# Scores of the second sequence and value products at other steps of TensorE's program

## Chip, cores and metric

The kernel runs on one core of one Trainium2 chip. The metric is the device time of one execution in microseconds (us), as the median of several runs. The profile is that of one further execution.

## The reference

A layer of a small transformer with 32 sequences of 256 tokens and width 128. A layer norm without scale feeds two branches whose results are added to `x`:

```
xn = layernorm(x)
h  = relu(xn @ nm_w1 + nm_b1);  m = h @ nm_w2 + nm_b2
q, k, v = m @ q_w + q_b, m @ k_w + k_b, m @ v_w + v_b
attention: softmax over the keys within 32 positions of the query, scale 1/sqrt(128)
scores = sigmoid(xn @ gate_w.T);  the 8 best of 16 experts by scores + expert_bias,
         their scores divided by their sum, times 2.826
y  = sum over experts of combine * (silu(xn @ w_gate.T) * (xn @ w_up.T)) @ w_down.T
y += the same for a shared expert, with weight 1
out = x + attention + y
```

All is float32. All 16 experts are computed for all tokens, and the combine weights of those not chosen are zero.

## The kernel before

**Tiles.** Tokens are worked in 16 groups of 512, two sequences each. Tensors lie transposed, 128 features on the partitions and 512 tokens along the row. To keep float32 precision each operand is split in two parts in TensorE's float32r type, `hi` (a copy that rounds) and `lo` (what is left), and each product is made of three, `PAIRS3`: hi by hi, hi by lo, lo by hi.

**Steps.** A group is 17 steps (`STEPS`), one for the shared expert and one for each of the 16. Each engine has its own program, written out by hand as `slot(g, par, s)`, and all five are tied by semaphores alone. The expert of step s goes through:
- PE (TensorE): gate product `ps_g` (L370, one step ahead), up product `ps_u` (L380), later the down product into `ps_y` (L390), `LAG` = 3 steps behind. Each is three products of 512 columns.
- ACT (ScalarE): `silu` of `ps_g` (L564), one step ahead; `h_hi` from `ps_u` (L572), one step behind.
- POOL (GpSimd): `silu_c`, the silu times the combine weight (L969).
- DVE (VectorE): `ps_u` times `silu_c` in place (L889) and `h_lo` (L895), one step behind.

There are two buffers each for `ps_g` and `ps_u`. So the gate product of step s waits for the silu of step s-2 (L368), and the up product of step s, called up(s) in the prediction, waits for `h_lo` of step s-2 (L378).

**The attention of the group** and the router and hidden layer of the next one are laid between these steps. On PE `att_early` stands between the gate product and the down product, `att_late` between the down product and the up product, and step 7 has something behind the up product. For this case they matter in this order:
- step 1: transposes of the next group's `xn` into `bank[1]`
- step 3: `scores(0)`, six products of 160 columns into `score_bank[0]` = `bank[2]`, with ahead of it the wait for `q_lo` (L459)
- step 4: `gate(1 - par)`, the router products of the next group, eight of 32 columns into `bank[0]` (L318), with ahead of it the waits for `xn_lo`, `hn_lo` and `key_term`
- step 5: `scores(1)`, the same into `score_bank[1]` = `bank[1]` (L329)
- step 7: four transposes of the probabilities of sequence 0 (L338), then the hidden projection of the next group (L306); step 9: the transposes of sequence 1
- step 13: `attend(0)`, step 14: `attend(1)`, the value products of the two sequences, six products of 160 or 256 columns each, into two halves of `bank[2]` (L348); the second raises `pv`

The other engines: DVE takes the row maximum of sequence 0 in step 4 and that of sequence 1 at the very start of step 6 (`row_max`, L810). ACT has in step 5 the exponential of the router and of sequence 0, in step 6, between `h_hi` of step 5 and the silu of step 7, the exponentials of sequence 1 (L553). Exponential and silu need a table load between them. DVE normalises the probabilities in steps 6 and 8 (L818, L822), ahead of that step's `h_lo`. ACT waits for `pv` in step 15 (`z_hi`, L547).

Of the kernel before, what the change touches and what calls it, by code (L numbers as in the profile page):

```python
# [64 lines left out]
def layer(nc, x, x_t, watt, watt_t, expert_bias, wexp, out_t, c_dram):  # L65
    ctx = ExitStack()
    with ctx:
# [6 lines left out]
        def sem(name):  # L74
            return ctx.enter_context(nc.semaphore(name))
# [120 lines left out]
        S = {n: sem(n) for n in names}  # L196
# [13 lines left out]
        def first(g):  # L210
            return g == 0

        def last(g, ahead=0):
            return g >= GROUPS - 1 - ahead
# [9 lines left out]
        def flat(t):  # L224
            return t[:].rearrange("p a d -> p (a d)")
# [75 lines left out]
        def _(pe):  # L301
# [7 lines left out]
            def turn(dst, src):  # L309
                for a in range(TILES):  # L310
                    done = nc.tensor.transpose(dst[:, a * P:(a + 1) * P], src[:, a * P:(a + 1) * P], ident[:])  # L311
                return done

            def gate(par):

                for a in range(TILES):
                    for n in range(2):
                        done = mm(bank[0][:, a * 2 * E:(a + 1) * 2 * E], xn_t[par][n][:, a * P:(a + 1) * P],  # L318
                                  gate_w[:], start=n == 0, stop=n == 1)
                done.then_inc(S["gate_mm"], 1)  # L320

            def scores(seq):

                dst = score_bank[seq]
                for t in range(2):
                    q0 = seq * SEQ + t * P
                    k0 = seq * SEQ + t * (P - HALF)
                    for n, (a, b) in enumerate(PAIRS3):
                        done = mm(dst[:, t * SEQ:t * SEQ + WIN], q_t[a][:, q0:q0 + P], hid_t[b][:, k0:k0 + WIN],  # L329
                                  start=n == 0, stop=n == 2)  # L330
                done.then_inc(S[f"sc{seq}"], 1)

            def turn_probs(seq):
                dst = score_bank[seq]
                for kb in range(2):
                    for t in range(2):
                        c = kb * (SEQ - (P - HALF)) + t * P
                        done = nc.tensor.transpose(dst[:, c:c + P],  # L338
                                                   prob_n[:, 2 * seq + t, kb * P:(kb + 1) * P], ident[:])
                done.then_inc(S[f"pt{seq}"], 1)  # L340

            def attend(seq):

                for kb in range(2):
                    col = seq * SEQ + kb * (P - HALF)
                    for n, (a, b) in enumerate(PAIRS3):
                        wide = SEQ if kb == 0 and n == 0 else WIN
                        done = mm(bank[2][:, col:col + wide], hid_n[a][:, seq * 2 + kb, :],  # L348
                                  p_t[b][:, seq, kb, 0:wide], start=kb == 0 and n == 0, stop=kb == 1 and n == 2,
                                  skip_group_check=True)  # L350
                return done

            def value_proj(g):

                pe.wait_ge(S["z_lo"], g + 1)
                for a, b in PAIRS3:
                    mm(ps_y[:], att_w[a][:, 2, :], z_t[b][:], start=False, stop=False, skip_group_check=True)  # L357
# [42 lines left out]
            def q_proj(g):  # L400
                pe.wait_ge(S["hid_lo"], g + 1)
                project(bank[1], 1, hid_t).then_inc(S["q_mm"], 1)

            def hid_turn(g):

                pe.wait_ge(S["hid_lo"], g + 1)
                turn(bank[0], hid).then_inc(S["hid_tp"], 1)
# [40 lines left out]
            def att_early(g, par, s):  # L448

                more = not last(g)  # L450
                if s == 1 and more:
                    pe.wait_ge(S["xn"], g + 2)

                    pe.wait_ge(S["q_lo"], g + 1)
                    turn(bank[1], flat(xn)).then_inc(S["xn_tp"], 1)
                if s == 3:
                    if not first(g):
                        pe.wait_ge(S["z_lo"], g)
                    pe.wait_ge(S["q_lo"], g + 1)  # L459
                    scores(0)  # L460
                if s == 4 and more:
                    pe.wait_ge(S["xn_lo"], g + 2)

                    pe.wait_ge(S["hn_lo"], g + 1)
                    pe.wait_ge(S["key_term"], 2 * g + 2)
                    gate(1 - par)
                if s == 5:
                    scores(1)
                if s == 15 and more:
                    q_proj(g + 1)  # L470
                if s == 16 and more:
                    hid_turn(g + 1)

            def att_late(g, par, s):

                if s == 0 and not first(g):
                    value_proj(g - 1)
                if s == 9:
                    pe.wait_ge(S["pn1"], g + 1)
                    turn_probs(1)  # L480
                if s == 13:
                    pe.wait_ge(S["hn_lo"], g + 1)
                    pe.wait_ge(S["p0_lo"], g + 1)
                    attend(0)
                if s == 14:
                    pe.wait_ge(S["p1_lo"], g + 1)
                    attend(1).then_inc(S["pv"], 1)

            def slot(g, par, s):
                if first(g) and s == 0:  # L490
                    gate_proj(g, par, s)
                if not (last(g) and s == STEPS - 1):
                    gate_proj(*after(g, par, s))
                att_early(g, par, s)
                if not first(g) or s >= LAG:
                    down(*before(g, par, s, LAG))
                att_late(g, par, s)
                up_proj(g, par, s)
                if s == 7:
                    pe.wait_ge(S["pn0"], g + 1)  # L500
                    turn_probs(0)
                    if not last(g):
                        hid_proj(g + 1, 1 - par)
# [510 lines left out]
```

## Time and profile before

| | us |
|---|---|
| median of 3 runs | 722.94 (722.91 to 723.25) |
| profiled execution | 722.1 |
| its span | 720.2 |
| PE busy | 701.5 (97% of the span) |
| DVE busy | 574.2 (80%) |
| ACT busy | 438.9 (61%) |
| POOL busy | 399.7 (55%) |

Busy time is the union of an engine's instructions. Products on PE are pipelined: one is shown with about 0.4 us, but the next begins 0.23 us after it. So the distance between starts tells what a product costs, and not its duration. Instructions of DVE and ACT overlap by about 0.1 us in the same way. In brackets behind an instruction stands how long its engine idled before it and which instruction ended that.

### The profile page before, as it was taken

What the parts mean: (1) busy time and instruction counts of PE and PEld (TensorE: products, weight loads), DVE (VectorE), ACT (ScalarE), POOL (GpSimd) and SP (SyncE); (2) the same over time, 40 slices, a digit from 0 to 9 for tenths busy, and PEclk for the clock granted to TensorE, in tenths of its full rate; (3) what the DMA queues carried; (4) which work ended last, traced back from release to release, by engine and by line L of the source; (5) the groups of instructions that cost most, each with busy time, mean ns of one, the idle gap of its engine ahead of it and who ended that gap; (6) DMA issues with size and microseconds to landing.
All of it is one profiled execution on the core that took longest, in us unless ns stands there. A gap on an engine that the chain in (4) does not pass through costs nothing.

```text
span 720.2 us, 10617 instructions
## 1 busy us (share of the span) xinstructions
PE 701.5 (97%) x3384; PEld 577.2 (80%) x3384; DVE 574.2 (80%) x1605; ACT 438.9 (61%) x874; POOL 399.7 (55%) x356
## 2 busy tenths in 40 slices
PE   5889999999999999999999999999999999999997
PEld 4667888888888888888888888888888888888886
DVE  4788788787888878788887888878787887878775
ACT  3575665666656575665766656566655766656573
POOL 3745555546565555565556655555565555655463
PEclk9999999999999999999999999999999999999999
DMA  7704316061250615216061340615215061430600
GB/s 256 256 10 152 130 26 226 29 235 45 90 191 2 234 45 177 103 47 218 16 235 45 109 172 4 236 42 204 76 51 227 4 236 45 130 135 7 244 1 15
DMA packets 36647, 84.72 MB, mean 118 GB/s; under 512 B 7152, under 2 KB 15472, under 8 KB 36592
## 3 DMA queue, kind: packets, MB, share of 16 engines
q1 hardware_dynamic: 36592, 84.05, 33.2%
q8 instruction: 27, 0.44, 0.3%
q14 instruction: 28, 0.23, 0.1%
HBM read 79.32 MB, written 4.72 MB: 117 GB/s over the span
## 4 chain that ended last, share of the span: by engine, by line
PE 93%; DVE 3%; DMA 2%; ACT 1%; issue 0%; POOL 0%; SPq 0%; DVEq 0%
PE ps_y L390 26%; PE ps_u L380 26%; PE ps_g L370 26%; PE bank L348 3%; PE bank L306 3%; PE bank L329 3%; PE bank L318 2%; PE bank L311 2%; PE bank L338 2%; PE ps_y L357 1%; DMA comb_b<-c_dram 1%; DVE ps_u L889 0%; DVE h_lo L895 0%; DVE exp_w_lo L644 0%; DMA xin<-x 0%
## 5 line engine op out<-in xcount | busy, mean ns | idle before, releaser
L969 POOL TENSOR_TENSOR silu_c<-silu,comb_b 128x512 f32<-128x512 f32 x256 | 330.5, 1294 | 300.7 <-ACT silu L564 297.1
L572 ACT ACTIVATE h_hi<-ps_u 128x512 fp32r<-128x512 f32 x272 | 162.5, 598 | 261.7 <-DVE ps_u L889 259.8
L895 DVE TENSOR_TENSOR h_lo<-ps_u,h_hi 128x512 fp32r<-128x512 f32 x272 | 185.7, 683 | 59.9 <-ACT h_hi L572 59.7
L889 DVE TENSOR_TENSOR ps_u<-silu_c,ps_u 128x512 f32<-128x512 f32 x256 | 176.6, 690 | 44.5 <-PE ps_u L380 38.2
L564 ACT ACTIVATE silu<-ps_g 128x512 f32<-128x512 f32 x272 | 161.4, 594 | 0.2
L380 PE MATMUL ps_u<-xn_hi,exp_w_hi 128*128 128x512 f32 x272 | 110.7, 407 | 5.1 <-DVE h_lo L895 5.1
L390 PE MATMUL ps_y<-h_hi,exp_w_hi 128*128 128x512 f32 x272 | 112.7, 414 | 0.4 <-DVE h_lo L895 0.4
L370 PE MATMUL ps_g<-xn_hi,exp_w_hi 128*128 128x512 f32 x272 | 108.3, 398 | 0.0
L370 PE MATMUL ps_g<-xn_lo,exp_w_hi 128*128 128x512 f32 x272 | 108.0, 397 | 0.0
L370 PE MATMUL ps_g<-xn_hi,exp_w_lo 128*128 128x512 f32 x272 | 107.6, 395 | 0.0
L380 PE MATMUL ps_u<-xn_lo,exp_w_hi 128*128 128x512 f32 x272 | 107.5, 395 | 0.0
L390 PE MATMUL ps_y<-h_hi,exp_w_lo 128*128 128x512 f32 x272 | 107.5, 395 | 0.0
L390 PE MATMUL ps_y<-h_lo,exp_w_hi 128*128 128x512 f32 x272 | 107.2, 394 | 0.0
L380 PE MATMUL ps_u<-xn_hi,exp_w_lo 128*128 128x512 f32 x272 | 107.2, 394 | 0.0
L380 PEld LDWEIGHTS ps_u<-xn_hi,exp_w_hi 128*128 128x128 f32 x272 | 51.3, 189 | 17.3 <-DVE h_lo L895 7.3
L370 PEld LDWEIGHTS ps_g<-xn_hi,exp_w_hi 128*128 128x128 f32 x272 | 51.4, 189 | 12.5 <-issue 0.3
L370 PEld LDWEIGHTS ps_g<-xn_hi,exp_w_lo 128*128 128x128 f32 x272 | 51.4, 189 | 12.4
L390 PEld LDWEIGHTS ps_y<-h_hi,exp_w_lo 128*128 128x128 f32 x272 | 51.0, 188 | 12.5
L380 PEld LDWEIGHTS ps_u<-xn_hi,exp_w_lo 128*128 128x128 f32 x272 | 51.1, 188 | 12.2
L370 PEld LDWEIGHTS ps_g<-xn_lo,exp_w_hi 128*128 128x128 f32 x272 | 51.3, 189 | 11.9
L380 PEld LDWEIGHTS ps_u<-xn_lo,exp_w_hi 128*128 128x128 f32 x272 | 51.4, 189 | 10.0
L390 PEld LDWEIGHTS ps_y<-h_hi,exp_w_hi 128*128 128x128 f32 x272 | 51.3, 189 | 9.5 <-DVE h_lo L895 0.8
(139 smaller groups left out, 982.0 us busy)
## 6 DMA issues: line engine op xcount, KB each, us to landing
comb_b<-c_dram SPq DMA_DIRECT2D x64, 1024.0 KB, 8.7
xin<-x SPq DMA_DIRECT2D x16, 256.0 KB, 3.1
xres<-x_t SPq DMA_DIRECT2D x16, 256.0 KB, 2.7
out_t<-xres SPq DMA_DIRECT2D x16, 256.0 KB, 2.0
exp_raw<-wexp SPq DMA_DIRECT2D x3, 960.0 KB, 9.3
c_dram<-comb_t SPq DMA_DIRECT2D x64, 8.0 KB, 1.8
exp_raw<-wexp SPq DMA_DIRECT2D x1, 384.0 KB, 5.4
att_raw<-watt SPq DMA_DIRECT2D x1, 330.5 KB, 3.4
```

The costliest lines, as they stand in the source:

```text
L306: done = mm(dst[:], att_w[a][:, w, :], parts[b][:], start=n == 0, stop=n == 2)
L311: done = nc.tensor.transpose(dst[:, a * P:(a + 1) * P], src[:, a * P:(a + 1) * P], ident[:])
L329: done = mm(dst[:, t * SEQ:t * SEQ + WIN], q_t[a][:, q0:q0 + P], hid_t[b][:, k0:k0 + WIN], start=n == 0, stop=n == 2)
L348: done = mm(bank[2][:, col:col + wide], hid_n[a][:, seq * 2 + kb, :], p_t[b][:, seq, kb, 0:wide], start=kb == 0 and n == 0, stop=kb == 1 a ...
L370: done = mm(ps_g[i][:], exp_w[a][:, s, 0:P], xn_t[par][b][:], start=n == 0, stop=n == 2)
L380: done = mm(ps_u[i][:], exp_w[a][:, s, P:2 * P], xn_t[par][b][:], start=n == 0, stop=n == 2)
L390: done = mm(ps_y[:], exp_w[a][:, s, 2 * P:3 * P], h_t[i][b][:], start=s == 0 and n == 0, stop=s == STEPS - 1 and n == 2, skip_group_check= ...
L564: A(silu[i][:], ps_g[i][:], ACT.Silu).then_inc(s_silu, 1)
L572: A(h_t[hbuf(par, s)][0][:], ps_u[(par + s) % 2][:], ACT.Copy).then_inc(s_h_hi, 1)
L889: V.tensor_tensor(ps_u[i][:], src[:], ps_u[i][:], ALU.mult).then_inc(s_h, 1)
L895: V.tensor_tensor(t[1][:], ps_u[(par + s) % 2][:], t[0][:].bitcast(F32), ALU.subtract)\
L969: G.tensor_tensor(silu_c[i][:].rearrange("p (l x) -> p l x", l=2), silu[i][:].rearrange("p (l x) -> p l x", l=2), comb_b[:, :, s1 - 1, :], ...
```

## The change

In PE's program `scores(1)` moves from step 5 to step 4, where it stands directly behind the router products of the next group. `attend(0)` moves from step 13 to step 14, with its two waits, and now stands directly ahead of `attend(1)`; the wait for `p1_lo` is made ahead of both. The other engines' programs are the same as before.

```
@@ att_early
                     pe.wait_ge(S["hn_lo"], g + 1)
                     pe.wait_ge(S["key_term"], 2 * g + 2)
                     gate(1 - par)
-                if s == 5:
+                if s == 4:
                     scores(1)
@@ att_late
-                if s == 13:
+                if s == 14:
                     pe.wait_ge(S["hn_lo"], g + 1)
                     pe.wait_ge(S["p0_lo"], g + 1)
+                    pe.wait_ge(S["p1_lo"], g + 1)
                     attend(0)
-                if s == 14:
-                    pe.wait_ge(S["p1_lo"], g + 1)
                     attend(1).then_inc(S["pv"], 1)
```

## Rows read from the trace of the kernel before

**Rows 1.** The page: busy us of an engine, and TensorE's granted clock in 40 slices

```profile
PE 701.5 (97%) x3384; PEld 577.2 (80%) x3384; DVE 574.2 (80%) x1605; ACT 438.9 (61%) x874; POOL 399.7 (55%) x356
PEclk9999999999999999999999999999999999999999
```

**Rows 2.** Who waited for whom: us in total, times, longest us

```profile
PE ps_u L380 <- DVE h_lo L895: 5.1, 5, 2.7
```

**Rows 3.** Timeline (start us, us, engine line, operation), PE, group 2, steps 4 and 5

```profile
124.89 0.39 PE L370 MATMUL ps_g<-xn_hi,exp_w_lo 128*128 128x512 f32 x1
...
126.24 0.40 PE L390 MATMUL ps_y<-h_lo,exp_w_hi 128*128 128x512 f32 x1
...
127.17 0.39 PE L380 MATMUL ps_u<-xn_hi,exp_w_lo 128*128 128x512 f32 x1
...
127.87 0.40 PE L370 MATMUL ps_g<-xn_hi,exp_w_lo 128*128 128x512 f32 x1
...
129.00 0.40 PE L390 MATMUL ps_y<-h_lo,exp_w_hi 128*128 128x512 f32 x1
```

**Rows 4.** Timeline, PE, around `attend(0)` in step 13 of group 2

```profile
147.59 0.40 PE L390 MATMUL ps_y<-h_hi,exp_w_lo 128*128 128x512 f32 x1
...
148.73 0.39 PE L380 MATMUL ps_u<-xn_lo,exp_w_hi 128*128 128x512 f32 x1
```

**Rows 5.** Timeline, DVE, group 2: product of step 4 to `h_lo` of step 8

```profile
127.60 0.69 DVE L889 TENSOR_TENSOR ps_u<-silu_c,ps_u 128x512 f32<-128x512 f32 x1 [0.83 <-PE ps_u L380]
...
129.57 0.32 DVE L810 CUSTOM_DVE_ANT_0 prob<-bank,mask_k 128x160 f32<-128x160 f32 x1
...
131.84 0.17 DVE L818 RECIPROCAL row_inv<-row_sum 128x2 f32<-128x2 f32 x1 [0.78 <-ACT prob L553]
...
132.48 0.68 DVE L895 TENSOR_TENSOR h_lo<-ps_u,h_hi 128x512 fp32r<-128x512 f32 x1
...
140.36 0.68 DVE L895 TENSOR_TENSOR h_lo<-ps_u,h_hi 128x512 fp32r<-128x512 f32 x1
```

**Rows 6.** Timeline, ACT, group 2: `h_hi` of step 4 to the silu of step 7

```profile
128.33 0.60 ACT L572 ACTIVATE h_hi<-ps_u 128x512 fp32r<-128x512 f32 x1 [1.79 <-DVE ps_u L889]
...
129.44 1.28 ACT L528 ACT_TABLE_LOAD   x1
130.73 0.26 ACT L528 ACTIVATE gate_e<-gate_s 128x64 f32<-128x64 f32 x1
...
134.43 0.60 ACT L564 ACTIVATE silu<-ps_g 128x512 f32<-128x512 f32 x1
```

**Rows 7.** Timeline, group 0: `h_lo` of step 8 ends and up(10) begins

```profile
54.65 0.68 DVE L895 TENSOR_TENSOR h_lo<-ps_u,h_hi 128x512 fp32r<-128x512 f32 x1
...
55.38 0.19 PEld L380 LDWEIGHTS ps_u<-xn_hi,exp_w_hi 128*128 128x128 f32 x1 [0.72 <-DVE h_lo L895]
...
55.72 0.39 PE L380 MATMUL ps_u<-xn_lo,exp_w_hi 128*128 128x512 f32 x1
```

**Rows 8.** Timeline, PE, group 2: up(7), gate product of step 9, up(10); up(7) of group 3

```profile
133.67 0.39 PE L380 MATMUL ps_u<-xn_hi,exp_w_hi 128*128 128x512 f32 x1
...
135.51 0.40 PE L370 MATMUL ps_g<-xn_hi,exp_w_hi 128*128 128x512 f32 x1
...
141.53 0.39 PE L380 MATMUL ps_u<-xn_hi,exp_w_hi 128*128 128x512 f32 x1
...
176.71 0.39 PE L380 MATMUL ps_u<-xn_hi,exp_w_hi 128*128 128x512 f32 x1
```

**Rows 9.** Timeline, group 0: end of up(4) and DVE's product of step 4

```profile
36.95 0.40 PE L380 MATMUL ps_u<-xn_hi,exp_w_lo 128*128 128x512 f32 x1
...
37.86 0.68 DVE L889 TENSOR_TENSOR ps_u<-silu_c,ps_u 128x512 f32<-128x512 f32 x1
```

**Rows 10.** Timeline, group 15: silu of step 7 and gate product of step 9

```profile
692.40 0.60 ACT L564 ACTIVATE silu<-ps_g 128x512 f32<-128x512 f32 x1
...
693.38 0.40 PE L370 MATMUL ps_g<-xn_lo,exp_w_hi 128*128 128x512 f32 x1
```

More of the change, by code:

```diff
@@ L466, in att_early @@
                     gate(1 - par)
-                if s == 5:
+                if s == 4:
                     scores(1)
@@ L480, in att_late @@
                     turn_probs(1)
-                if s == 13:
+                if s == 14:
                     pe.wait_ge(S["hn_lo"], g + 1)
                     pe.wait_ge(S["p0_lo"], g + 1)
+                    pe.wait_ge(S["p1_lo"], g + 1)
                     attend(0)
-                if s == 14:
-                    pe.wait_ge(S["p1_lo"], g + 1)
                     attend(1).then_inc(S["pv"], 1)
```

## The prediction

> **What bounds the kernel now.** I read the page first: PE is busy for 701.5 us of the 720.2 us span, at a granted clock of 9 tenths or more in every slice, that is at the higher of its two levels, 2.4 GHz [rows 1]. Then I read who waits for whom. PE's only repeated wait is for `h_lo` of L895, before an up product: 5 times, 5.1 us [rows 2], and the timeline puts all five of them in group 0. From group 1 to group 14 the products follow each other without a hole. So PE's program order sets the time, and an edit there can act in two ways: by making the sum of PE's work shorter, or by opening a hole where an operand comes too late. The third view is therefore the timeline of one middle group (group 2), PE beside DVE and ACT. Steps are called s as in the code. The start of a product in a stalled or narrow place is taken as the start of the next product less 0.233 us, the spacing of wide (512 column) products: from 127.17 to 127.87 there are three spacings, 0.70 us [rows 3].
>
> **Part 1, PE's own work.** Nothing is added or removed: six narrow products per sequence for scores and six for values, in another place. What could change is the edge between wide and narrow products, since two blocks of 8 and 6 become one of 14, and two of 6 become one of 12. The eight router products: from the last wide start before them (124.89) to the second wide start behind them (126.24) is 1.35 us, less two wide spacings (0.467) makes 0.883. The six of the scores: 127.87 to 129.00 is 1.13, less 0.467 makes 0.663 [rows 3]. The two extra products cost 0.220, or 0.110 each; six at 0.110 leave 0.003 for the edges. Value products: 147.59 to 148.73 is 1.14, less 0.467 makes 0.673 [rows 4], of which 6 x 0.110 leaves 0.013. An edge thus costs between nothing and about 0.015 us. Two edges less in 16 groups give 0 to 0.5 us; I take 0, as a difference of rows rounded to 0.01 can't carry more.
>
> Here a rule of the Trainium skill can be weighed. "TensorE: Matmul & The Clock Gate", section "Back-to-back issue gap", gives a sustained spacing of about 81 ns for products of 128 columns. By it six narrow products would take an estimated 0.49 us, and the sum below would come out at about 725.7 instead of 728.4 (rival C). The rows show 0.110 us each, whether the product has 32 or 160 columns, so the rule does not hold for these float32 operands.
>
> **Part 2, what the moved scores delay.** In step 4 the order becomes gate product of step 5, the eight router products, scores(1), down of step 1, up of step 4. So up(4) ends 0.66 us later. Step 5 gets the same 0.66 us shorter, so the gate product of step 6 starts 0.66 later, and up(5) and all of PE behind it start as now. scores(1) itself adds no wait in this place: the semaphores that it relies on have been waited for by scores(0) and by the router products. Its own reader, the row maximum of sequence 1, stands in DVE's step 6 and starts at 129.57 with no wait ahead of it, behind `h_lo` of step 4 [rows 5]; it comes by DVE's order and not by the scores' end, so nobody gains from having them early.
>
> Who waits for up(4) is what counts. DVE's product of step 4 starts at 127.60 after 0.83 us of idleness that up(4) ended [rows 5]; up(4) ends at 127.17 + 0.39 [rows 3]. So it moves by the whole 0.66, to 128.26. ACT's `h_hi` of step 4 starts at 128.33 after 1.79 us of waiting for that DVE product, and moves to 128.99. Behind it ACT has no hole up to silu(7): silu(6), a table load, the exponentials of both sequences with `h_hi` of step 5 between them, a second table load, silu(7) at 134.43 [rows 6]. ACT is in order, so silu(7) ends at 135.03 + 0.66 = 135.69. On DVE the probabilities of sequence 0 wait for the exponentials (131.84, 0.78 us idle), and `h_lo` of step 5 (132.48, ends 133.16) [rows 5] stands behind them: it ends at 133.82. From there DVE has at most short holes, each ended by ACT or by POOL, which itself waits for silu(7), up to `h_lo` of step 10. So `h_lo` of step 8 (ends 141.04) [rows 5] is 0.66 later too.
>
> Another rule of the Trainium skill speaks of the table loads. "ScalarE: Activation LUTs", section "What ACT_TABLE_LOAD costs", adds a drain of about 1380 ns to every load. By it ACT would have no slack to PE at all, and all 0.66 us would come through in each group (rival B). The row shows 1.28 us from 129.44 and the next instruction at 130.73 [rows 6], so no drain is seen.
>
> **Part 3, how much slack PE has.** Where PE really waited, in group 0, `h_lo` ended at 55.33, the weight load began at 55.38, and the second product at 55.72, so the first counts from 55.49: an operand must be there 0.16 us before the product's start [rows 7]. With that, from group 2:
> - up(7) starts at 133.67 [rows 8], its operand is free at 133.16: slack 0.51 - 0.16 = 0.35.
> - gate product of step 9 starts at 135.51 [rows 8], silu(7) ends at 135.03: 0.48 - 0.15 = 0.33.
> - up(10) starts at 141.53 [rows 8], `h_lo` of step 8 ends at 141.04: 0.49 - 0.16 = 0.33.
> - By the same working up(8), up(9), up(11) and up(12) have 0.42 to 0.50; up(13) has 1.24, and the up products of steps 14 to 6 have at least 1.1.
>
> A delay of 0.66 is larger than the first three. PE stops before up(7) for 0.31, before the gate product of step 9 for another 0.02, and then stands at 0.33, which also covers the rest: the hole is the largest single excess, not their sum. Nothing gives it back, as PE has no other idle time in the group. DVE and ACT catch up in steps 13 to 16, where they idle waiting for PE, so nothing is carried to the next group. Groups 1 to 14: 14 x 0.33 = 4.6 us.
>
> Group 0: DVE's product of step 4 starts at 37.86, after up(4) ended at 37.35 [rows 9], so 0.51 less a 0.03 us handover is hidden and about 0.18 arrives. Up(7) to up(10) are already late there, so it all shows: 0.2. Group 15: the gate product of step 9 already waits for silu(7) (692.40 + 0.60; second product 693.38, so the first counts from 693.15) [rows 10]: no slack, 0.66. Sum 4.6 + 0.2 + 0.7 = 5.5 us.
>
> **Part 4, the value products.** attend(0) leaves step 13 and stands ahead of attend(1) in step 14. Up(13), the gate product of step 15 and down(11) start 0.67 earlier, up(14) and all behind as now. The reader, ACT's copy `z_hi`, waits for both sequences, whose end doesn't move. I cost this at nothing, covered by slack: up(13) keeps 1.24 - 0.67 = 0.57, the other two have over 2 us. With the DVE chain 0.66 late and PE 0.33 late it keeps 0.24. Without that cover it would cost at most what is missing, 0.1 us in each group for each 0.1. A gain has nowhere to go, as DVE and ACT are not what PE waits for in steps 14 to 16.
>
> **Sum.** Profiled run 722.1 us, 720.2 of span and 1.9 around it. Predicted span 725.7, profiled run 727.6; the runs shown have a median of 722.94, so 728.4 us, 0.76% slower.
>
> **The rivals.**
> - A, forecast: excess over the slack, 728.4. If the handover of 0.16 is off by 0.05, 14 groups give 0.7 either way; if group 0 passes on all of 0.66, 0.5 more. Own range 727.0 to 730.0. Chance 0.72.
> - B, all the 0.66 arrives in each group (the slack is already used by something that the rows don't show, such as a weight load that must be issued earlier): 16 x 0.66 = 10.6, 733.5. Against it: in group 2 nothing waits. Chance 0.06.
> - C, half arrives: ACT or DVE takes up part of the delay in the table loads or exponentials, or the merged block is shorter than its parts. With 0.5 instead of 0.66 late: 14 x 0.17 + 0 + 0.5 = 2.9, 725.8. Chance 0.10.
> - D, the other side: a fixed price per edge between wide and narrow that my difference doesn't see. At one narrow spacing, 0.11 us, for each of the 2 blocks removed in 16 groups it gives 3.5 us, and if the delay is hidden as well, 719.4. It decides the sign only from (5.5 + 1.4) / 32 = 0.22 us per block when the delay is as I say, or 0.045 when it is hidden. The rows show 0.003 and 0.013 [rows 3, 4]. Chance 0.04.
> - E, the move changes nothing that PE waits for, because the slack from up(4) to up(7) is 0.66 or more after all: 722.9. Against it: three separate operands have 0.33 to 0.35. Chance 0.08.
>
> A measurement of this kernel tells about 0.2%, 1.4 us, from no change. Faster 0.04 (D), same 0.08 (E), slower 0.88 (A, B, C). A, with C on the lower and a part of B on the upper side, gives the range: 725.2 to 731.0.
>
> **What would show it.** In the changed kernel a wait of PE for `h_lo` of L895 before up(7), and for the silu before the gate product of step 9, in each of groups 1 to 14, together 0.3 us a group; a group spacing, from one up(7) to the next, of 43.37 instead of 43.04 us (133.67 to 176.71) [rows 8]; ACT's first `h_hi` of the long stretch 0.66 later against PE's router products; router and score products with 0.11 us each over the merged block of 14; no wait at all in steps 13 to 16. The forecast is wrong if PE stays without holes, or if the merged blocks take less than 14 x 0.11 and 12 x 0.11 us.

## The result, and the profile after

The changed kernel takes 728.81 us (median of 4, 728.08 to 728.98) beside 723.1 for the kernel before: a ratio of 1.0075, with a 95% interval of 1.0057 to 1.0092. The forecast was 728.4, in a range of 725.2 to 731.0. The profiled execution has a span of 726.9 us against 720.2.

Lines below L486 of the kernel before are one lower in the changed one: `h_lo` L894, product L888, silu L563, `h_hi` L571. First the page of the changed kernel, busy us of each engine:

```profile
PE 706.4 (97%) x3384; PEld 574.7 (79%) x3384; DVE 572.7 (79%) x1605; ACT 437.4 (60%) x874; POOL 399.5 (55%) x356
```

Against [rows 1] this looks harmless. PE is as busy as before at 97%, and its sum has grown by 4.9 us with the same 3384 products, where the span has grown by 6.7. Most of the loss thus hides in the busy time: a product is drawn with 0.4 us while the next may begin after 0.23, so a hole of a few tenths behind a product is largely drawn over. It shows in the weight loads (PEld) and in the distance of starts. Who waited for whom (us in total, times, longest us), first one row of the kernel before, then the changed kernel:

```profile
PEld ps_u L380 <- DVE h_lo L895: 7.3, 5, 3.1
```

```profile
PEld ps_u L380 <- DVE h_lo L894: 16.2, 33, 3.1
...
PE ps_u L380 <- DVE h_lo L894: 5.0, 4, 2.7
...
PEld ps_g L370 <- ACT silu L563: 3.5, 15, 0.7
```

PE's own row is that of [rows 2], one time fewer. The weight loads tell the rest: 33 waits for `h_lo` and not 5, and 15 for the silu. By the timeline each of groups 1 to 14 has three of them: 0.50 us at up(7), 0.20 at the gate product of step 9, 0.16 at up(10). The timeline of group 2 of the changed kernel (start, us, engine line, operation), from the end of the router products to the gate product of step 9:

```profile
126.22 0.39 PE L370 MATMUL ps_g<-xn_hi,exp_w_lo 128*128 128x512 f32 x1
...
128.24 0.40 PE L390 MATMUL ps_y<-h_lo,exp_w_hi 128*128 128x512 f32 x1
...
129.60 0.69 DVE L888 TENSOR_TENSOR ps_u<-silu_c,ps_u 128x512 f32<-128x512 f32 x1 [1.50 <-PE ps_u L380]
...
130.33 0.60 ACT L571 ACTIVATE h_hi<-ps_u 128x512 fp32r<-128x512 f32 x1 [2.46 <-DVE ps_u L888]
...
134.48 0.68 DVE L894 TENSOR_TENSOR h_lo<-ps_u,h_hi 128x512 fp32r<-128x512 f32 x1
...
135.22 0.19 PEld L380 LDWEIGHTS ps_u<-xn_hi,exp_w_hi 128*128 128x128 f32 x1 [0.49 <-DVE h_lo L894]
...
135.55 0.40 PE L380 MATMUL ps_u<-xn_lo,exp_w_hi 128*128 128x512 f32 x1
...
136.43 0.60 ACT L563 ACTIVATE silu<-ps_g 128x512 f32<-128x512 f32 x1
...
137.08 0.19 PEld L370 LDWEIGHTS ps_g<-xn_hi,exp_w_hi 128*128 128x128 f32 x1 [0.21 <-ACT silu L563]
```

The rows stand 1.33 us later than before at the start of the group, from the loss of groups 0 and 1. Less that, DVE's product of step 4 moved from 127.60 [rows 5] to 128.27, so 0.67 late; `h_hi` from 128.33 to 129.00; silu(7) from 134.43 [rows 6] to 135.10; `h_lo` of step 5 from 132.48 to 133.15. DVE waited 1.50 us for up(4) instead of 0.83, ACT 2.46 instead of 1.79, each 0.67 more. The chain of the work that ended last (start, us, what) was PE for 93% of the span before and is PE for 82% now. In group 2 it leaves PE behind up(4):

```profile
128.87 0.71 PE ps_u L380 x3
129.58 0.02 issue
129.60 0.70 DVE ps_u L888
130.31 0.02 issue
130.33 0.60 ACT h_hi L571
130.93 0.49 ACT silu L563
131.42 0.02 issue
131.44 1.28 ACT L527
132.73 0.03 ACT gate_e L527
...
134.36 0.12 issue
134.48 0.69 DVE h_lo L894
135.17 0.04 issue
135.22 0.96 PE ps_u L380 x3
```

Read from up(4), over DVE, ACT's silu, the table load (L527) and the exponentials, to `h_lo` of step 5 and up(7): this is the way that the prediction describes. ACT's silu in this chain is that of step 6.

**Where the time went, group by group.** I took the start of the second product of every up product in both traces and subtracted. In groups 1 to 14 the difference behaves the same each time: 0.67 more at up(4), back to its old value at up(5), 0.325 more at up(7), 0.026 more at up(8), 0.67 less at up(13) and back at up(14). Per group 0.356 us stay (0.33 to 0.37). Group 15 adds 0.68, group 0 adds 0.98. Together 14 x 0.356 + 0.68 + 0.98 = 6.6 us, the 6.7 of the spans. The 0.98 of group 0 is more than belongs to the change: most of it is a fall of the granted clock, told in the last section.

### The profile page after: what moved, and what is told of

It reads as the page before. It is cut to its first block, busy times and chain, and to the rows that moved or that the text cites. A ratio compares the mean times of both kernels' runs of the same rounds, so it can differ in the third digit from the quotient of the medians.

```text
span 726.9 us, 10617 instructions
## 1 busy us (share of the span) xinstructions
PE 706.4 (97%) x3384; PEld 574.7 (79%) x3384; DVE 572.7 (79%) x1605; ACT 437.4 (60%) x874; POOL 399.5 (55%) x356
## 4 chain that ended last, share of the span: by engine, by line
PE 82%; ACT 8%; DVE 6%; DMA 2%; issue 1%; SPq 0%; POOL 0%; DVEq 0%
PE ps_u L380 23%; PE ps_y L390 21%; PE ps_g L370 21%; PE bank L329 3%; PE bank L348 3%; PE bank L306 3%; ACT L527 3%; ACT prob L552 2%; PE bank L318 2%; PE bank L311 2%; PE bank L338 2%; DVE ps_u L888 2%; DVE h_lo L894 2%; ACT h_hi L571 2%; PE ps_y L357 1%
## 5 line engine op out<-in xcount | busy, mean ns | idle before, releaser
L571 ACT ACTIVATE h_hi<-ps_u 128x512 fp32r<-128x512 f32 x272 | 162.8, 598 | 269.8 <-DVE ps_u L888 269.8
L894 DVE TENSOR_TENSOR h_lo<-ps_u,h_hi 128x512 fp32r<-128x512 f32 x272 | 185.8, 683 | 59.8 <-ACT h_hi L571 59.6
L888 DVE TENSOR_TENSOR ps_u<-silu_c,ps_u 128x512 f32<-128x512 f32 x256 | 176.6, 690 | 47.5 <-PE ps_u L380 41.0
L563 ACT ACTIVATE silu<-ps_g 128x512 f32<-128x512 f32 x272 | 161.9, 596 | 0.2
L390 PEld LDWEIGHTS ps_y<-h_lo,exp_w_hi 128*128 128x128 f32 x272 | 51.5, 189 | 9.5
```

Source lines behind the costliest of these rows:

```text
L390: done = mm(ps_y[:], exp_w[a][:, s, 2 * P:3 * P], h_t[i][b][:], start=s == 0 and n == 0, stop=s == STEPS - 1 and n == 2, skip_group_check= ...
L563: A(silu[i][:], ps_g[i][:], ACT.Silu).then_inc(s_silu, 1)
L571: A(h_t[hbuf(par, s)][0][:], ps_u[(par + s) % 2][:], ACT.Copy).then_inc(s_h_hi, 1)
L888: V.tensor_tensor(ps_u[i][:], src[:], ps_u[i][:], ALU.mult).then_inc(s_h, 1)
L894: V.tensor_tensor(t[1][:], ps_u[(par + s) % 2][:], t[0][:].bitcast(F32), ALU.subtract)\
```

## Experiments

**Each half alone.** First only the scores, then only the value products:

```
e1_scores_only                      e2_values_only
-                if s == 5:         -                if s == 13: ... attend(0)
+                if s == 4:         +                if s == 14: ... attend(0)
                     scores(1)                            attend(1)
```

> Only scores(1) moves from step 5 to step 4; the value products stay as in the kernel before. Theory A (the excess of the 0.66 us delay of up(4) over PE's slack): the whole loss is here, 728.4 to 728.9, with a wait of PE before up(7) and before the gate product of step 9 in groups 1 to 14, 0.35 us a group. Rival F (the loss comes from the block of twelve value products, or from both moves together): under 727. Side question, group 0: if the fall of the granted clock to its lower level behind the 2.7 us hole belongs to the moved scores, it is seen here again.

> Only attend(0) moves from step 13 to step 14. Theory A: no difference, 723.1 within 0.5, and the spacing of groups stays at 43.03 us. Rival D (a fixed price per edge between wide and narrow products): 0.11 us a group less, 721.3. Rival F: over 724.

Measured: e1 728.4 us (727.4 to 729.2, ratio 1.0079, interval 1.0066 to 1.0092), e2 722.83 (ratio 1.0007, interval 0.9998 to 1.0016), beside 722.7 for the kernel before. Per group of 1 to 14 the traces give 0.336 us for e1 and 0.001 for e2. Who waited for whom in e1:

```profile
PEld ps_u L380 <- DVE h_lo L895: 16.1, 33, 3.1
...
PEld ps_g L370 <- ACT silu L564: 3.4, 15, 0.7
```

The same 33 and 15 waits as in the changed kernel. The loss is that of the scores; the value products cost and bring nothing by themselves, though up(13) starts 0.68 us earlier in each group. Rival F falls by both runs, and rival D by e2, which is not at 721.3.

**Adjacent, but without delaying up(4).** The block of fourteen stands behind the up product:

```
 e3_block_behind_up, from the changed kernel
                 att_late(g, par, s)
                 up_proj(g, par, s)
+                if s == 4:
+                    ... the three waits and gate(1 - par) of att_early, unless last(g)
+                    scores(1)
```

> As the changed kernel, but the block of eight router products and six score products stands behind up(4) and not ahead of the down product. The two are as adjacent as in the changed kernel, but up(4) now starts 0.88 us earlier than in the kernel before. Theory A: the gate product of step 6 ends 0.66 later, so ACT's silu of step 6 starts about 0.13 later, less than the slack of 0.33: no wait in groups 1 to 14, 722.5 to 723.3. Rival G (that the products are adjacent is itself what costs: one block of 14, or two PSUM banks filled right after another): 728 to 729.

Measured: 723.47 us (722.72 to 723.79), ratio 1.001, interval 1.0001 to 1.0019; I had expected 723.3 at most. All but 0.8 us of the loss is gone while the products are as adjacent as in the changed kernel, so rival G falls. In e3 the reason for ACT's start has changed too, as forecast: it now waits for the delayed gate product of step 6, once in each of 14 groups:

```profile
ACT silu L562 <- PE ps_g L370: 13.1, 14, 0.9
```

`h_lo` of step 5 is 0.15 us later relative to its group and not 0.67. There remain 0.027 us a group (below) and 0.19 in group 15.

**The dose.** Part of scores(1) in step 4, the rest in step 5: three products, then five. `scores` takes the part as a further argument.

```
 e4_half_early                        e5_five_early
+                if s == 4:          +                if s == 4:
+                    scores(1, (0,)) +                    scores(1, 0, 5)
                 if s == 5:                           if s == 5:
-                    scores(1)       -                    scores(1)
+                    scores(1, (1,)) +                    scores(1, 5, 6)
```

> The kernel before with half of scores(1), the three products of its first tile, in step 4 and the other half in step 5: up(4) is 0.33 us late and not 0.66. Theory A (threshold at a slack of 0.33 to 0.35): groups 1 to 14 show 0 to 0.03 us each, group 15 0.33, together 0.3 to 0.8: 723.4 to 723.9. Rival B (all of a delay arrives): 16 x 0.33 = 5.3, 728.4. Rival H (the loss is in proportion to the delay): half, 725.9.

> The kernel before with five of the six products of scores(1) in step 4 and the last in step 5: up(4) is 0.55 us late. Theory A with a slack of 0.33 and a slope of one behind it: PE waits 0.22 to 0.24 us in each of groups 1 to 14, 0.55 in group 15 and 0.1 in group 0, together 3.9 us: 726.6. Rival J (past the threshold the whole delay arrives, since PE then runs against the chain of the other engines): 14 x 0.55 + 0.6 = 8.3, 731. Rival K (the loss comes only with the complete early sequence, as its row maximum or its bank then changes hands earlier): 723.

Measured: e4 723.13 us (ratio 1.0001, interval 0.9992 to 1.001), e5 726.45 (ratio 1.0049, interval 1.0036 to 1.0061; before 722.62). From the traces, means over groups 1 to 14:

| kernel | up(4) later, us | group longer, us |
|---|---|---|
| e4 | 0.333 | 0.003 |
| e5 | 0.549 | 0.216 |
| e1 | 0.675 | 0.336 |
| changed kernel | 0.674 | 0.356 |

The slack comes out as 0.33 in e5 (0.549 - 0.216) and 0.34 in e1 (0.675 - 0.336), and the excess arrives one for one. This sets aside B (all of it arrives), H (in proportion), J and K at once, and the part of C in which ACT or DVE takes up some of the delay. Rival E fell with the result itself. In e4 the weight loads already wait. Group 2 of e4:

```profile
134.36 0.19 PEld L381 LDWEIGHTS ps_u<-xn_hi,exp_w_hi 128*128 128x128 f32 x1 [0.16 <-DVE h_lo L898]
...
136.23 0.19 PEld L371 LDWEIGHTS ps_g<-xn_hi,exp_w_hi 128*128 128x128 f32 x1 [0.18 <-ACT silu L567]
```

Such waits of 0.16 and 0.18 us cost nothing: a group of e4 is 0.003 us longer. They are the first sign that the slack is used up. My forecast for e4 was 723.4 to 723.9. The median is below it; the 0.33 of group 15 is there in the trace, but the runs don't resolve it.

**The way taken out.** ACT's exponentials become the identity, which leaves out exp and the two table loads of a group; in the changed kernel and in the kernel before.

```
 e6_after_no_exp, e7_before_no_exp
-                    done = A(prob[:, n, :], prob[:, n, :], ACT.Exp, scale=-1.0,
+                    done = A(prob[:, n, :], prob[:, n, :], ACT.Identity, scale=-1.0,
 and the same in gate_exp
```

> The changed kernel with ACT's two exponentials (router and attention) replaced by the identity, which needs no other table: this leaves out exp and both table loads of a group, so the output is not the reference's, while all products, waits and sizes stay. ACT's stretch from h_hi of step 4 to silu of step 7 gets 2.6 us shorter. Theory A (the delay travels through this stretch): PE no longer waits in groups 1 to 15, and the time is within 0.5 us of the next kernel, the same edit in the kernel before. Rival L (the delay reaches PE over DVE alone, by h_lo of steps 4 and 5): the difference to that kernel stays at 5 us or more.

> The kernel before with the same identity in place of the exponentials, as the partner of the run above; exp and both table loads of a group are left out. Theory A: groups 1 to 14 are as long as before, 43.03 us, since PE waits for nothing there; groups 0 and 15 lose part of their holes: 719.5 to 723.

Measured: 720.23 us (719.59 to 720.33) and 719.78 (719.16 to 720.03), 0.45 apart instead of 5.7. With the move in place up(4) is still 0.676 late in every group, and yet a group is only 0.026 longer. So the delay reaches PE through the stretch of ACT that holds the exponentials and the table loads; rival L falls. e7 keeps its groups 1 to 14 to 0.00 us as they were: in the kernel before, the exponentials cost nothing but slack. In e6 the weight loads wait for `h_lo` 5 times and not 33:

```profile
PEld ps_u L380 <- DVE h_lo L894: 5.6, 5, 1.9
```

**Group 0, and a better kernel.** In the kernel before, up(8) of group 0 stands still for 2.68 us. Its operand, `h_lo` of step 6, waits in DVE's queue behind the low parts of the experts' weights and the router. The rows, group 0 of the kernel before:

```profile
46.13 1.34 DVE L644 TENSOR_TENSOR exp_w_lo<-exp_raw,exp_w_hi 128x384 fp32r<-128x384 f32 x1 [1.71 <-ACT exp_w_hi L520]
47.39 1.25 DVE L681 TENSOR_SCALAR gate<-gate_e 128x64 f32<-128x64 f32 x1
...
49.41 0.68 DVE L895 TENSOR_TENSOR h_lo<-ps_u,h_hi 128x512 fp32r<-128x512 f32 x1
...
50.15 0.50 PE L380 MATMUL ps_u<-xn_hi,exp_w_hi 128*128 128x512 f32 x1 [2.68 <-DVE h_lo L895]
```

```
 e8_weights_later (from the kernel before), e9_after_weights_later (from the changed one)
-                if first(g) and 0 < s <= STEPS - EARLY:
-                    expw_lo(s + EARLY - 1)
+                if first(g) and (0 < s <= 5 or 10 <= s <= 13):
+                    expw_lo(s + EARLY - 1 if s <= 5 else s + 3)

 e10_weights_later_still (from the kernel before)
+                if first(g) and (0 < s <= 5 or s in (10, 12, 13, 14)):
+                    expw_lo(s + EARLY - 1 if s <= 5 else (s + 3 if s == 10 else s + 2))
```

> The kernel before; only in group 0 DVE makes the low parts of the last four experts' weights in steps 10 to 13 and not in steps 6 to 9, where PE stands still for 2.7 us before up(8). If the hole is DVE's queue in steps 6 and 7 (h_lo of step 6 starts at 49.41 though its operand is there at 46.6), 1.5 to 2.8 us go: 720 to 721.3. It also tells about the granted clock in group 0, which fell to its lower level behind the hole at 50 us in the changed kernel and in four experiments with and without a loss: theory M (it falls after that hole) expects no fall here; rival N (it falls at this time of the run whatever PE did before) expects it again.

> The changed kernel with the weights of group 0 made later on DVE, as in the run before this one. Theory A: the loss of groups 1 to 15 (14 x 0.356 + 0.68 = 5.7) has nothing to do with group 0 and stays whole, while group 0 gains the 2.7 us of its hole: about 725.2, that is 5.7 above the kernel with later weights alone. Rival O: part of the loss was a loss of group 0 (a longer hole, a fall of the granted clock): clearly less than 725. Theory M again: no fall of the granted clock in group 0.

> The kernel before with the low parts of the last four experts' weights made in steps 10, 12, 13 and 14 of group 0. The run with steps 10 to 13 kept two holes of PE, 0.7 and 0.4 us of waiting in the weight loads of up(11) and up(12), each for an h_lo that stands behind such a weight on DVE. With none in step 11 the second of them should go: 718.9 to 719.3.

Measured: e8 719.31 us (718.76 to 719.7), ratio 0.995, interval 0.9938 to 0.9963, below both kernels and below the 720 to 721.3 that I expected. The same place in e8:

```profile
46.60 0.69 DVE L895 TENSOR_TENSOR h_lo<-ps_u,h_hi 128x512 fp32r<-128x512 f32 x1 [1.24 <-ACT h_hi L572]
...
47.34 0.19 PEld L380 LDWEIGHTS ps_u<-xn_hi,exp_w_hi 128*128 128x128 f32 x1 [0.34 <-DVE h_lo L895]
```

`h_lo` of step 6 now starts when its operand is there, at 46.60 and not at 49.41, and all that follows is 2.66 us earlier. The medians differ by 3.3: most executions of the kernel before also lose about 1 us by the fall of the clock, and none of e8 does (last section).

e9 took 725.64 us (725.25 to 725.69), 6.3 above e8; I had expected 5.7. The two ran on different chips; against the kernel before on its own chip e8 is 3.3 less and e9 2.8 more, 6.1 apart. The trace of e9 gives 14 x 0.363 + 0.68 + 0.5 for group 0. The loss of the later groups is thus independent of group 0, and rival O falls. The 0.5 of group 0 is not the scores' doing. From up(7) to up(12) the two traces differ by 0.02 or less, since the 0.2 that the scores take meets a start that is 0.2 earlier; the 0.5 arises at up(13), which gains only 0.19 us by the moved `attend(0)` and not 0.67. The row, group 0 of e9, where e8 has no such wait:

```profile
59.46 0.19 PEld L380 LDWEIGHTS ps_u<-xn_hi,exp_w_hi 128*128 128x128 f32 x1 [0.64 <-DVE h_lo L894]
```

So moving `attend(0)` is not always free: in this group `h_lo` of step 11 stands on DVE behind a late weight, up(13) has no slack to use the earlier place, and up(14) pays for it.

e10 took 719.65 us, not less than e8 (on another chip): a miss. Its trace is 0.35 us longer too. The hole of up(12) went, but a larger one came, since the weights of step 14 were now themselves late. Group 0 of e10:

```profile
56.84 1.05 DVE L644 TENSOR_TENSOR exp_w_lo<-exp_raw,exp_w_hi 128x384 fp32r<-128x384 f32 x1
...
57.94 0.19 PEld L370 LDWEIGHTS ps_g<-xn_hi,exp_w_hi 128*128 128x128 f32 x1 [0.89 <-DVE exp_w_lo L644]
```

## Why the prediction was right, and where it was off

**The path.** Part 2 held link by link: up(4), DVE's product, `h_hi`, ACT's stretch, silu(7) and `h_lo` of step 5, each about 0.67 late. e6 shows that the stretch with the exponentials carries it, e3 that being adjacent doesn't.

**The size of the slack.** Forecast 0.35 before up(7) and 0.33 before the gate product of step 9, from the handover of 0.16 us in group 0 [rows 7, 8]. Measured 0.33 to 0.34 by the dose. PE's excess is 0.325 at up(7) and 0.026 at the gate product of step 9, where I had 0.31 and 0.02. The rule "the largest excess, not the sum" held; up(10) and the others added nothing that stays.

**Groups 0 and 15.** Group 15: forecast 0.66, measured 0.68. Group 0: forecast 0.18 for what arrives at DVE and ACT. In the changed kernel `h_lo` of step 5 lost 0.18 there against `h_lo` of step 4, and in e5, with a delay of 0.55, group 0 as a whole lost 0.10 as its expectation said. The 0.98 of the changed kernel is that 0.2, plus 0.96 to 0.97 from the fall of the clock, less 0.2 by which its group 0 already ran earlier up to step 4 in this profile. e2 and e3, which hardly lose anything, have 0.64 and 0.65 in group 0 of their profiles in the same way.

**The sum.** 14 x 0.356 + 0.68 + 0.2 = 5.9 us from the traces, 5.7 from the medians, 5.5 forecast. Of the terms, that of groups 1 to 14 came out 0.4 larger than forecast (5.0 for 4.6), most of it by the price of the joined blocks, told next (from e1 to the changed kernel 14 x 0.020).

**The term that had the wrong sign.** In part 1 I gave the edges between wide and narrow products 0 to 0.5 us as a gain and took 0. With both blocks joined there is no gain but a small loss where nothing waits: 0.027 us a group in e3, and 0.026 between e6 and e7, some 0.4 us in all; 0.020 between e1 and the changed kernel. e2 alone shows 0.001, and the block of fourteen itself measures 2.02 - 0.467 = 1.55 us (126.22 to 128.24 in the rows above) against 0.883 + 0.663 = 1.546 apart. In the traces of the changed kernel, e3 and e6 about 0.01 us of it arises between up(3) and up(5) and 0.014 to 0.018 between up(12) and up(14), the second part only where the scores have moved too. Why it arises stays open. My bound should have reached below nothing as well.

**The value products.** Forecast nothing, with up(13) keeping enough slack. e2: 0.001 us a group; the changed kernel has no wait in steps 13 to 16. The cover is needed, as the prediction says: in group 0 of e9 it was not there, and 0.5 us were lost.

**The rules of the Trainium skill.** The Trainium skill gives about 81 ns for a narrow product ("TensorE: Matmul & The Clock Gate", "Back-to-back issue gap"), and by it the sum would have been an estimated 725.7. e1 shows up(4) 0.675 us late for six products, 0.11 each. The Trainium skill puts a drain of about 1380 ns behind a table load ("ScalarE: Activation LUTs", "What ACT_TABLE_LOAD costs"), and by it the sum would have been an estimated 733.5. In the chain above the instruction behind the 1.28 us load follows 0.01 us later. In both places the measurement decides against the rule for this kernel.

## What to carry to other kernels

When the bounding engine has no hole, list for each of its steps how much earlier than needed the operand is there, and compare every reordering with that list: the excess over the smallest slack on the way is lost in each round, and what stays below it costs next to nothing (0.003 us a group in e4). A block moved ahead of a product delays everything that hangs on that product, even if the engine's own sum of work is the same; put behind it, the same block cost 0.8 us in all and not 5.7. Look at the idle time of the weight loads and at the distance of starts, since the busy share of the products stayed at 97% with 5.7 us lost.

## What the runs showed that I had not expected

In group 0 the granted clock of PE fell to its lower level, 1.2 GHz, shortly behind the hole of 2.7 us before up(8). The page of the profile doesn't show it: a slice there is 18 us, and every one has a 9 in both kernels. Windows (stretch, length, then busy us of PE, PEld, DVE, ACT, POOL, granted clock as a share of 2.4 GHz, DMA share, GB/s) of the kernel before, of the changed kernel, then of e2:

```profile
50.00:52.00 2.00, 1.85 (x8) 1.54 (x9) 1.96 (x10) 1.27 (x3) 0.04 (x1) 1.00 0.00 0
```

```profile
50.00:52.00 2.00, 1.86 (x6) 1.53 (x7) 1.96 (x10) 1.28 (x3) 0.05 (x1) 0.72 0.00 0
52.00:54.00 2.00, 2.00 (x8) 1.52 (x7) 2.00 (x6) 0.91 (x3) 1.23 (x1) 0.50 0.00 0
54.00:56.00 2.00, 2.00 (x11) 1.69 (x10) 2.00 (x12) 0.87 (x3) 1.29 (x1) 0.92 0.00 0
```

```profile
50.00:52.00 2.00, 2.00 (x5) 1.61 (x6) 1.97 (x10) 1.50 (x3) 0.39 (x1) 0.50 0.00 0
52.00:54.00 2.00, 2.00 (x10) 1.58 (x10) 2.00 (x8) 1.02 (x2) 0.90 (x1) 0.69 0.00 0
```

It lasted some 3 us and put PE back by about 1.0 us: up(10) of group 0 stands 0.96 us later against up(8) in the changed kernel than in the kernel before. Of the seven profiles that have the 2.7 us hole, five show the fall (changed kernel, e1, e2, e3, e4) and two don't (kernel before, e5). Of the five in which the hole before up(8) is 1.2 us or less (e6 to e10) none does, and there the clock is 1.00 in this stretch.

The mean granted clock on record for every execution says the same with larger numbers, though not where in the execution a fall stands. It is 0.997 or 0.998 in the profiles with the fall, and 0.999 or 1.000 in those without. Among the executions of kernels with the 2.7 us hole it is 0.998 or less in 67 of 92, and in 34 of 45 of the kernel before by itself: these 34 have a median of 722.9 us, the other 11 one of 721.9. In the 25 executions of e6 to e10 it is never below 0.999. So the fall doesn't belong to the change. It comes in most executions behind the hole but not in all, and e8, which is the kernel before without the hole, never has it, nor has e9 at the same time of its run. Rival N (the fall comes at this time whatever PE did) falls with that, and theory M stands; why the fall stays out in a quarter of the executions is not known. It explains most of why the spans of the two profiles differ by 6.7 us where the medians differ by 5.7: the profile of the kernel before is one without it.
